# Second attention of a two-layer block: exponentials over three PSUM banks instead of two

## The reference, cut to what matters

```python
attn = jnp.einsum('bhqd,bhkd->bhqk', q, k) * scale
attn = attn + alibi
attn = jnp.where(causal, attn, jnp.finfo(x.dtype).min)
p = jax.nn.softmax(attn, axis=-1)
out = jnp.einsum('bhqk,bhkd->bhqd', p, v).transpose(0, 2, 1, 3).reshape(b, t, c)
return out @ Wo + bo
```

## Time and profile before

| | |
|---|---|
| median of 3 runs | 874.09 us (873.14 to 874.2) |
| the profiled execution's own time | 875.88 us |
| its span, first to last instruction | 874.2 us |
| granted TensorE clock over the span | 0.986 |
| busy: PE, ACT, DVE, POOL | 786.2, 823.8, 420.2, 222.9 us |
| exponentials of the second attention (L1966) | 288, 267.4 us busy, 594.5 to 865.7 us |

### The profile page before, as it was taken

One profiled execution on the slowest core, in us unless ns is written; L12 is line 12 of the kernel. 1 busy time (PEld: TensorE's weight loads), 2 busy tenths in 40 slices (PEclk: granted clock), 3 DMA queues, 4 the chain that ended last, 5 costly groups with the idle time before them and its releaser, 6 DMA issues.

```text
span 874.2 us, 21888 instructions
## 1 busy us (share of the span) xinstructions
PE 786.2 (90%) x9230; PEld 302.1 (35%) x9230; DVE 420.2 (48%) x892; ACT 823.8 (94%) x917; POOL 222.9 (25%) x268
## 2 busy tenths in 40 slices
PE   3869999899999999999999999997988978988986
PEld 2422433234343433433343433223333323323322
DVE  7931265473657652677537588996021121121122
ACT  7679999999999999999999996769999999999996
POOL 5301110130212041111303021203334334334333
PEclk9969999999999999999999999998999999999999
DMA  6793020100210300203000016100203112022000
GB/s 189 285 283 58 2 78 3 61 18 2 78 51 1 127 2 23 82 25 115 13 3 25 26 45 210 39 25 1 67 13 90 41 50 90 15 77 90 13 1 25
DMA packets 31947, 53.43 MB, mean 61 GB/s; under 512 B 5480, under 2 KB 16360, under 8 KB 31848
## 3 DMA queue, kind: packets, MB, share of 16 engines
q1 hardware_dynamic: 31848, 52.01, 18.9%
HBM read 31.29 MB, written 20.71 MB: 59 GB/s over the span
## 4 chain that ended last, share of the span: by engine, by line
PE 73%; ACT 17%; DVE 4%; issue 4%; DMA 1%; PEldq 0%; PEld 0%; SPq 0%; ACTq 0%; DVEq 0%
PE c_ps L1263 27%; PE c_ps L1246 13%; ACT c_ring L1966 11%; PE c_ps L112 10%; PE c_ps L2159 8%; PE c_ps L2120 8%; ACT c_ring L1003 3%; PE c_ps L615 1%; PE c_ps L1681 1%; DVE early L1626 1%; PE c_ps L1696 1%; ACT xs L1973 1%; PE c_ps L1688 1%; ACT c_ring L1484 1%; PE c_ps L606 1%
## 5 line engine op out<-in xcount | busy, mean ns | idle before, releaser
L1003 ACT ACTIVATE c_ring<-c_ps 128x1024 f32<-128x1024 f32 x512 | 473.3, 1033 | 4.2 <-PEq L1227 2.9
L1263 PE MATMUL c_ps<-c_ring,vt 128*18 128x256 f32 (+1 forms) x3072 | 271.6, 456 | 0.0
L1966 ACT ACTIVATE c_ring<-c_ps 128x1024 f32<-128x1024 f32 x288 | 267.4, 1070 | 1.1 <-PE c_ps L2120 0.7
L2159 PE MATMUL c_ps<-c_ring,vt 128*18 128x512 f32 (+3 forms) x1664 | 152.5, 468 | 2.0 <-issue 0.9
L1246 PE MATMUL c_ps<-q_st,k_st 32*128 32x512 f32 x1016 | 129.5, 498 | 19.9 <-ACT c_ring L1003 18.9
L1991 POOL TENSOR_SCALAR_AFFINE_SELECT c_ring<-c_ring 128x512 f32<-128x512 f32 x128 | 84.5, 679 | 173.6 <-ACT c_ring L1966 173.1
L1263 PEld LDWEIGHTS c_ps<-c_ring,vt 128*18 128x18 f32 x3072 | 64.9, 97 | 142.5 <-issue 102.5
L2120 PE MATMUL c_ps<-q_st,k_st 32*128 32x512 f32 (+3 forms) x768 | 80.0, 416 | 34.0 <-ACT c_ring L1966 30.2
L1246 PEld LDWEIGHTS c_ps<-q_st,k_st 32*128 32x128 f32 x1016 | 49.8, 182 | 135.4 <-ACT c_ring L1003 132.5
L1024 POOL TENSOR_TENSOR early<-early 128x512 f32<-128x512 f32 x32 | 38.4, 1201 | 176.3 <-DVE early L1147 176.3
L2120 PEld LDWEIGHTS c_ps<-q_st,k_st 32*128 32x128 f32 x768 | 39.8, 185 | 108.2 <-ACT c_ring L1966 99.0
(11 more groups left out here) (248 smaller groups left out, 776.3 us busy)
## 6 DMA issues: line engine op xcount, KB each, us to landing
q_st<-q_hl SPq DMA_DIRECT2D x48, 256.0 KB
k_st<-k_hl SPq DMA_DIRECT2D x48, 256.0 KB
q_hl<-parts SPq DMA_DIRECT2D x10, 512.0 KB, 4.4
k_hl<-parts SPq DMA_DIRECT2D x10, 512.0 KB, 4.7
q_hl<-c_ring SPq DMA_DIRECT2D x4, 512.0 KB, 3.7
k_hl<-c_ring SPq DMA_DIRECT2D x4, 512.0 KB, 4.4
out_dram<-x SPq DMA_DIRECT2D x7, 256.0 KB, 4.2
x<-in_L_attn_x_dram SPq DMA_DIRECT2D x3, 512.0 KB, 5.7
```

Source lines behind the costliest of these rows:

```text
L1003: nc.scalar.activation(probs[t % RING][:, 2 * pair:2 * pair + 2, :], scores[unit % SLOTS][:, :, :], ACT.Exp).then_inc(expd, 1)
L1263: ins = nc.tensor.matmul(o_ps[32 * h:32 * h + 2 * W9, c0:c1], vt[b % 2][:, kt, gp, h, W9 * gs:W9 * gs + 2 * W9], probs[t % RING][:, h, c0: ...
L1966: nc.scalar.activation(probs[t % RING][:, first:first + 2, :], scores[unit % SLOTS][:, :, :], ACT.Exp).then_inc(expd, 1)
L2159: ins = nc.tensor.matmul(o_ps[32 * h:32 * h + 2 * W9, q0:q0 + w], vt[b % 2][:, kt, gp, h, W9 * gs:W9 * gs + 2 * W9], probs[t % RING][:, h, ...
```

## The change

The exponential now covers three banks: a unit is three tiles (`WIDE = 3`, 128x1536), 192 units in all, and the scores have two slots of three banks. Four units make three steps, so two units of every four hold heads of two steps. `score` now takes a unit, and waits for the exponential of unit u - 2. The ring is counted in `TILES = 18` tiles, and a step's four tiles can lie around its end; there the mask takes two instructions for each column block (`spans`). The products are whole, and lag by three steps (`LAG1 = 3`). Side pieces stand between a unit's scores and a product. `th1`, a buffer of the middle, now lies in the ring's last four tiles, so unit 5 waits for `twisted[1]`. The clearing of the bank for `o_ps`, now another bank, stands between the two last twists.

```diff
+TILES = 18
@@ the middle, DVE @@
-        dve.wait_ge(*room["freed"][0])
-        nc.vector.memset(room["o_ps"], 0.0).then_inc(room["o_clear"], 1)
         twist(ROUNDS - 1, 0)
+        dve.wait_ge(*room["freed"][2])
+        nc.vector.memset(room["o_ps1"], 0.0).then_inc(room["o_clear"], 1)
         twist(ROUNDS - 1, 1)
...
-LAG1 = 2
+LAG1 = 3
...
+WIDE = 3
+def last_unit(t):
+    return (G * t + G - 1) // WIDE
+def spans(t):
+    first = G * t % TILES
+    if first + G <= TILES:
+        return [(first, first + G)]
+    return [(first, TILES), (0, first + G - TILES)]
...
@@ act_part @@
+        for u in range(UNITS):
...
+            if u == TILES // WIDE - 1:
+                act.wait_ge(twisted[1], 2 * CYCLES)
+            if WIDE * u >= TILES:
+                act.wait_ge(pv_done, (WIDE * u + WIDE - 1 - TILES) // G + 1)
+            act.wait_ge(scored, u + 1)
+            at = WIDE * u % TILES
+            nc.scalar.activation(probs[:, at:at + WIDE, :], wide[u % 2], ACT.Exp).then_inc(expd, 1)
...
@@ mask @@
+                for first, last in spans(t):
+                    part = probs[:, first:last, n * P:(n + 1) * P]
...
@@ pe_part @@
+        def score(u):
+            if u >= 2:
+                pe.wait_ge(expd, u - 1)
...
+            for t in range(WIDE * u // G, (WIDE * u + WIDE - 1) // G + 1):
...
+                places = [at for at in range(G) if (G * t + at) // WIDE == u]
+                banks = {order[at]: wide[u % 2][:, (G * t + at) % WIDE, :] for at in places}
...
+            ins.then_inc(scored, 1)
...
-        for pair in range(LAST):
...
+        for t in range(S + LAG1):
+            if t < S:
+                score(4 * (t // 3) + t % 3)
+            for one in pieces_at(t // 2) if t % 2 == 0 else ():
+                piece_of(*one)
+            if t >= LAG1:
+                product(t - LAG1)
+            if t < S and t % 3 == 2:
+                score(4 * (t // 3) + 3)
...
-        ring = sb("ring", [P, RING * G, HALF])
+        ring = sb("ring", [P, RING * G + 4, HALF])
...
+            "tiles": ring[:, 0:TILES, :], "wide": [banks[:, 4:7, :], banks[:, 0:3, :]], "o_ps1": banks[:, 3, :],
```

More of the change, by code:

```diff
@@ L1900, in second_attention @@
     q_st, k_st, vt, on = s["q_st"], s["k_st"], s["vt"], s["on"]
-    probs = room["ring"]
+    probs, wide = room["tiles"], room["wide"]
     turn = [s["ext"][0][:, HALF * n:HALF * n + HALF] for n in range(2)]
@@ L1906, in second_attention @@
     twisted, kept_xt = room["twisted"], room["kept"]
-    o_ps, side = room["o_ps"], room["side"]
-    scores = [room["scores"][n] for n in (2, 0, 1)]
+    o_ps, side = room["o_ps1"], room["side"]
     side_tiles = side[:, :].rearrange("p (t c) -> p t c", c=C)
-    tail_banks = [scores[t // 2][:, t % 2, 0:C] for t in range(HT)]
+    tail_banks = [wide[t // 2][:, t % 2, 0:C] for t in range(HT)]
     staged = s["staged"][1]
@@ L1955, in act_part @@
     def act_part(act):
-        for t in range(S):
-            b, r = divmod(t, PER1)
-            if t == 2:
+        for u in range(UNITS):
+            first, last = WIDE * u // G, (WIDE * u + WIDE - 1) // G
+            if u == 2:
                 act.wait_ge(twisted[0], 2 * CYCLES)
[L1960 to L1973, removed]
+            if u == TILES // WIDE - 1:
[5 more added lines that the diff above has]
+            nc.scalar.activation(probs[:, at:at + WIDE, :], wide[u % 2], ACT.Exp).then_inc(expd, 1)
+            for t in range(first, last + 1):
+                b, r = divmod(t, PER1)
+                for hf in range(2):
+                    if r == TANH_AT[hf] and last_unit(t) == u:
+                        act.wait_ge(side_in, fill_index("z", b, hf) + 1)
+                        if b > 0:
+                            act.wait_ge(gated, 2 * (b - 1) + hf + 1)
+                        nc.scalar.activation(th[hf][:, :, :], s["y"][:, tiles(b, hf), :], ACT.Tanh, scale=0.5).then_inc(th_rdy, 1)
     def pool_part(pool):
@@ L2094, in pe_part @@
     def pe_part(pe):
-        def score(t, places=range(G)):
-            b, r = divmod(t, PER1)
[L2097 to L2156, removed]
@@ new lines, in product @@
+        def product(t):
+            b, r = divmod(t, PER1)
+            gp, qh, pieces, columns, opens, closes = plan[r]
+            order = head_order(plan[r])
+            if columns:
+                pe.wait_ge(masked, masked_count(t))
+            else:
+                pe.wait_ge(expd, last_unit(t) + 1)
+            if t == 0:
+                pe.wait_ge(o_clear, 1)
+            if opens and t > 0:
+                pe.wait_ge(o_free, ENDS * b + closing.index(next(c for c in closing if c >= r)))
+            if b > 1 and r == 0:
+                pe.wait_ge(v_rdy, b - 1)
@@ L2157, in product @@
             for n, (gs, kt, q0, at, w) in enumerate(pieces):
                 for h in range(G):
+                    tile = (G * t + order.index(h)) % TILES
                     ins = nc.tensor.matmul(o_ps[32 * h:32 * h + 2 * W9, q0:q0 + w],
[L2160 to L2161 removed]
@@ L2162, in product @@
-            if last:
-                ins.then_inc(pv_done, 1)
+                                           vt[b % 2][:, kt, gp, h, W9 * gs:W9 * gs + 2 * W9], probs[:, tile, at:at + w],
+                                           start=opens, stop=closes and n == len(pieces) - 1, tile_position=(0, 32 * h))
+            ins.then_inc(pv_done, 1)
         def piece_of(n, kind, b, hf, piece, pieces):
```

57 lines of the change are left out of this document (33 added, 24 removed).

## The result

The changed kernel takes **885.21 us**, median of 4 runs (883.18 to 887.08), against 873.62 for the kernel before beside it (4 runs, 873.04 to 874.2): a ratio of **1.0132 [1.0107, 1.0158]**. It is slower; 887 was predicted. Its profiled execution took 883.18 us, 7.3 more than that of before.

A forecast was written before the change was run, and what follows sets the result against it. ACT's exponentials were taken to bound the stage: 191 x 1.342 + 1.51 + 8 x 0.51 + 9.4 + 12.7 + 2.1 = 286.1, less 1.7, is 284.4 against 271.2. Adding 13.2 to 874.09 gave 887 us, range 874 to 894.

The forecast's parts named there:

- rival A: Exponential stage: ACT stays fed because the loop has more room than counted; -4.7 us, 869 us, chance 0.10.
- ACT's own work: Exponentials on ACT: 192 three-bank units, 1.342 us apart, take 258 us where 288 took 264; 6 us saved.
- (1): Units with heads of two steps, 8 of a batch's 12 cycles: pieces cost PE 0.24 us more, using up the reserve.
- reserve: Extra PE work that a plain cycle of four units takes up before ACT waits: 0.19 us.
- the third term: The forecast's loss from side pieces on PE between scores and a product: 12.7 us.
- (2): Cycles with cap matmuls on PE: exponentials 0.8 and 0.54 us late, 1.34 a cycle, 9.4 us for seven cycles.
- (3): Side pieces on PE between scores and a product: a mix or v costs 0.57, a z about 0.4; 12.7 us.
- (4): Stage's head: unit 5 waits for the last twist, at least 1.5 us, plus 0.6 for the lower clock: 2.1 us.
- (5): Ring wait and masks, selects around the ring's end taken as 1.6 us: all hidden, costing ACT nothing.
- C: Masks on POOL late: four half-size selects take 2.44 us, products wait 0.7, 16 times; +11, 898 us, chance 0.07.
- D: Scores on PE: heads of two steps in a unit don't lie side by side; some 30 us, 917 us, chance 0.03.
- B: Half of the losses, since pieces and caps lie beside products more than shown: stage 273, 876 us, chance 0.10.

The follow-up runs named there:

- e2: The changed kernel without the cap matmuls, the exponent scaled by 0.001: 874.82 us, 1.0002 of the kernel before.
- e3: The changed kernel with DVE's first gate one pair of steps later, behind the lift of o_ps: 878.81 us, 1.0051 of the kernel before.
- e4: The changed kernel with the scores of each cycle's fourth unit ahead of the third product: 876.53 us, 1.0034 of the kernel before.
- e10: The changed kernel with e3, e4, e6, capless scores first, side pieces before the fourth unit's scores, r = 0's behind the first unit: 870.59 us, 0.9957 of before.
- e1: The changed kernel run again unaltered, as a base: 881.97 us, 1.0094 of the kernel before.
- e6: The changed kernel with unit 5 no longer waiting for the second half's last twist: 885.02 us, 1.0128 of the kernel before.
- e5: The changed kernel with all side pieces of a cycle gathered behind the fourth unit's scores: 889.08 us, 1.018 of the kernel before.

## Why the prediction held, and where it was off

**The sign and the mechanism** were right: two slots of three banks leave so little room that what stands ahead of a refill on PE is waited for. e2, e3 and e4 each took waits away and got about the expected time back; rival A (ACT stays fed, 869) fell with them, though e10 comes within 2 us of its number, in another order of PE's work.

**The size.** The stage grew by 7.8 us and not 13.2. Of the 5.4 too many, 4.2 are late starts (18.3 instead of 22.5) and 1.2 the pitch (1.336 measured where 1.342 was worked out, 191 times). ACT idled 12.8 us, less than the 15 to 25 that were to show it. That the medians lie 11.6 apart, nearer to the forecast, is luck and no merit of the sum: the profiled executions lie 7.3 apart, and the kernel before ran 2.3 us above its median in its own, the changed one 2.0 below. On another chip e1 shows 7.8 between medians.

**ACT's own work**: 1.336 is 0.420 more than the 0.916 of two banks, between the 0.426 that was taken and the 0.41 of the Tanh. 288 x 0.916 - 192 x 1.336 = 7.3 us saved, 6 predicted. By the overlap of about 93 ns that the Trainium skill, page "ScalarE: Activation LUTs", section "What ACT_TABLE_LOAD costs", states, the estimate was 8.9 us saved; the run's 7.3 lies between it and the 6. A unit inside an unbroken stretch lasts 1.50 (626.81), one that waited 1.45, where 1.51 and 1.44 were taken.

**(1) Mixed units, the step that failed.** PE's timeline, two mixed units, each with a product behind it:

```profile
636.71 0.50 PE L2142 MATMUL c_ps<-q_st,k_st 32*128 32x512 f32 x5
637.14 1.06 PE L2165 MATMUL c_ps<-c_ring,vt 128*18 128x384 f32 x16
638.13 0.51 PE L2142 MATMUL c_ps<-q_st,k_st 32*128 32x384 f32 x5
638.57 0.63 PE L2165 MATMUL c_ps<-c_ring,vt 128*18 128x256 f32 x8
```

The unit of 638.13, five matmuls of two shapes, gives way after 0.44, like any other. The 0.24 were not there; the lower bound, nothing, was right. So eight cycles of a batch kept their reserve, which the third term had spent.

**(2) Caps**: predicted 1.34 a cycle, 9.4 in all and the eighth in the head; measured 8.0 over all eight, 7.7 without it, and 7.15 gained by e2. PE's timeline of one U2 with both caps:

```profile
665.90 0.44 PE L2142 MATMUL c_ps<-q_st,k_st 32*128 32x384 f32 x2
666.27 0.22 PE L2133 MATMUL c_ps<-mask_kq,ident_bf 128*128 128x96 bf16 x1
666.42 0.33 PE L2142 MATMUL c_ps<-q_st,k_st 32*128 32x128 f32 x2
666.68 0.22 PE L2133 MATMUL c_ps<-mask_kq,ident_bf 128*128 128x96 bf16 x1
666.82 0.50 PE L2142 MATMUL c_ps<-q_st,k_st 32*128 32x256 f32 x2
667.25 1.05 PE L2165 MATMUL c_ps<-c_ring,vt 128*18 128x512 f32 x8
```

From 665.90 to 667.25 are 1.35 us, 1.36 by the working: the pieces were sized well. The exponentials behind were 0.42 to 0.71 and 0.54 late, where 0.80 and 0.54 stood.

**(3) Side pieces, mis-sized most**: 5.3 us, 12.7 predicted. Two things: the reserve of (1), and their price on PE's timeline:

```profile
652.04 0.65 PE L112 MATMUL c_ps<-wo_x,on 128*32 128x128 f32 x16
652.50 1.04 PE L2165 MATMUL c_ps<-c_ring,vt 128*18 128x512 f32 x8
...
690.38 0.44 PE L2177 MATMUL c_ps<-ident,y 128*128 128x128 f32 x2
690.76 1.06 PE L2165 MATMUL c_ps<-c_ring,vt 128*18 128x256 f32 x16
```

A `mix` ahead of a product costs 0.46; the earlier trace rows gave 0.57 for one ahead of scores. A `z` costs 0.38, about 0.4 as said. So two `mix` exceed the reserve by some 0.66 to 0.73 and not 0.95 to 1.19, and the cycles with one `z` by almost nothing.

**(4) The head**: 2.0 without its capped cycle and 2.4 with it, 2.1 predicted. How much of this is the twist and how much PE at the lower clock stays open; e6 shows that the twist alone does not decide it.

**(5) Hidden**: ring and masks were. C (masks late) is refuted by e3, with 0.3 us for POOL, once. The selects on half the tiles take:

```profile
L2010 POOL TENSOR_SCALAR_AFFINE_SELECT c_ring<-c_ring 128x256 f32<-128x256 f32 x64 | 23.7, 407 | 12.6 <-ACT c_ring L1983 12.6
```

Four are 1.63 us (1.6 taken; 2.44 was C's). D (two heads of different steps apart) is refuted by every plain unit, at 0.44. B (half of the losses, 876) had 273 for the stage, 6 us under the 279.0 and so about as far off as my own 284.4. Its reason came in part: a `mix` beside a product costs 0.11 less than its row showed, the caps cost what theirs did.

**Not foreseen**: the lift behind the gate. The `z` at r = 18 and 20 were counted as 0.34 a batch of work on PE; the 0.74 a batch that came are a wait on DVE. Lag three moved the half's last product later, and so the lift, past the gate's place on DVE: I followed PE's and ACT's orders and not DVE's.

## What to carry to other kernels

A wider instruction that costs a buffer slot trades a small fixed saving (here 7 us) against the room of the loop; count that room as latest minus earliest start of the refill, per cycle, and the same work that was as good as free with three slots (caps: nothing that the runs can show) costs 7 us with two. Put the refill of a slot ahead of everything that nobody waits for: that order was worth 5.4 us here, and with the gate moved as well the wider form wins by 0.2%. When a lag changes, follow each engine that the lagging work feeds: a small transpose behind another engine's answer cost 3 us.

## What the runs showed that I had not expected

- Scores of two heads in two pieces with a third head's behind take 0.44 us, as three whole ones.
- In the waits, a weight load named POOL for 7.0 us that were DVE's.
- The granted clock fell after the lift's wait in e1, which it didn't in the changed kernel's first profile. The windows ahead of, at and after the fall in e1, and below them the first two places in the first profile, where the stage began 2.3 us later:

```profile
631.00:634.00 3.00, 1.54 (x21) 0.61 (x17) 2.08 (x4) 3.00 (x4) 2.45 (x4) 1.00 0.79 253
634.40:637.60 3.20, 3.20 (x30) 1.36 (x34) 0.00 (x0) 1.67 (x3) 0.86 (x2) 0.55 0.00 0
638.00:645.00 7.00, 6.31 (x75) 2.14 (x67) 2.54 (x5) 6.64 (x6) 1.48 (x4) 0.99 0.01 4
```

```profile
633.20:636.20 3.00, 1.54 (x21) 0.65 (x17) 1.88 (x4) 3.00 (x4) 2.25 (x3) 1.00 0.82 276
636.60:640.00 3.40, 3.40 (x49) 1.52 (x45) 0.00 (x0) 2.97 (x3) 1.07 (x2) 1.00 0.02 6
```

In e1, after 3 us in which PE was busy 1.54, the clock was 0.55 for 3.2 us, near the lower level (1.2 GHz), PE busy throughout and ACT only 1.67; then 0.99, near the higher (2.4 GHz). In the first profile PE was busy the same 1.54 of 3 us, and the clock stayed at 1.00. e6 showed the fall once, e2 once and for longer, e5 three times, each time behind the lift's wait. In e1 it made the late starts of the cycles of r = 21 some 1.5 us longer than in the first profile (4.5 against 3.0). Why the clock falls in one execution and not in another stays open.

- The changed kernel lies 11.6 us above before on one chip, 7.8 on the next and 11.2 (e6, nearly the same kernel) on a third. The runs' own mean granted clock goes with their time: in e1's six runs from 0.989 at 881.81 to 0.983 at 885.02, and the four behind the 885.21 have 0.984 and 0.980. Some of it lies ahead of the changed stage, whose first exponential starts at 591.5 us in e1's profile and at 593.8 in the first. So the clock fits these differences, but no run shows why it is lower in one place than in another.
